# A decoder layer's attention loop with one PSUM bank for both heads' turned probabilities and two for the projections

## The reference

```
x = x + attn(layernorm(x))        # rmsnorm inside, 16 heads of 64, softmax in fp32, output projection + bias
x = x + xattn(ctx, ctx, layernorm(x))   # one head of 128: q from x, k and v from the context, softmax, Wo + bo
x = x + ffn(layernorm(x))         # 128 -> 512 -> 128, relu; uint8 activations, int8 weights per channel

quant_act_uint8(x):    s = max(max(x), 1e-8) / 255;  round(x / s) clipped to 0..255, times s
quant_weight_int8(w):  s per row = max(|w|) / 127;   bias rounded to multiples of s_in * s_w
```

## Time and profile before

| | |
|---|---|
| runs | 414.09, 414.68, 415.33 us; median 414.68 |
| profiled execution | 414.31 us, its span 412.1 us |
| busy | PE 376.0 (91%), DVE 320.0 (78%), ACT 260.4 (63%), POOL 161.0 (39%) |
| one middle batch | 44.5 us, from like rows of neighbouring batches |
| first scores of the batches' loop, last output projection | 14.4 us, 366 us |
| TensorE's granted clock | 1.00 in all middle batches; half for some 3 us in the first batch and for stretches after 382 us |

### The profile page before, as it was taken

One profiled execution on the slowest core, in us unless ns is written; L12 is line 12 of the kernel. 1 busy time (PEld: TensorE's weight loads), 2 busy tenths in 40 slices (PEclk: granted clock), 3 DMA queues, 4 the chain that ended last, 5 costly groups with the idle time before them and its releaser, 6 DMA issues.

```text
span 412.1 us, 9065 instructions
## 1 busy us (share of the span) xinstructions
PE 376.0 (91%) x2989; PEld 289.1 (70%) x2989; DVE 320.0 (78%) x779; ACT 260.4 (63%) x814; POOL 161.0 (39%) x177
## 2 busy tenths in 40 slices
PE   1799999999999999999999999999999989987746
PEld 1677877687767876887768777787678767765115
DVE  3587778877987798859887798779885979847883
ACT  3676567675657665766767665766576656825762
POOL 1255534453454353534445345435353443401000
PEclk9989999999999999999999999999999999999659
DMA  7400000001000010001000100001000000000003
GB/s 241 128 15 2 0 2 2 1 3 40 2 0 3 0 40 0 0 0 38 0 0 0 38 0 0 0 0 38 0 0 0 25 2 2 2 2 0 0 0 103
DMA packets 12310, 7.50 MB, mean 18 GB/s; under 512 B 1280, under 2 KB 11264, under 8 KB 12288
## 3 DMA queue, kind: packets, MB, share of 16 engines
q1 hardware_dynamic: 11856, 6.69, 5.5%
q10 hardware_dynamic: 432, 0.52, 0.4%
HBM read 6.16 MB, written 1.05 MB: 18 GB/s over the span
## 4 chain that ended last, share of the span: by engine, by line
PE 75%; DVE 10%; issue 8%; POOL 3%; ACT 2%; DMA 1%; DVEq 0%; POOLq 0%; ACTq 0%
PE o_bank L467 14%; PE pT L458 12%; PE score L448 12%; PE acc_bank L474 6%; PE q_bank L431 6%; PE q_bank L433 3%; PE q_bank L432 3%; PE side_bank L431 3%; PE side_bank L525 3%; PE side_bank L432 2%; PE side_bank L433 2%; DVE h_max L1211 2%; DVE negmax L889 2%; POOL rstd L1245 2%; PE side_bank L521 2%
## 5 line engine op out<-in xcount | busy, mean ns | idle before, releaser
L1254 POOL TENSOR_TENSOR prob<-prob,rinv 128x512 f32<-128x512 f32 x128 | 132.5, 1044 | 178.6 <-DVE rinv L893 178.6
L707 ACT ACTIVATE prob<-score,negmax 128x256 f32<-128x256 f32 x252 | 117.1, 475 | 79.1 <-DVE negmax L889 78.3
L889 DVE TENSOR_REDUCE negmax<-score 128x2 f32<-128x512 f32 x126 | 80.9, 683 | 43.7 <-PE score L448 43.6
L896 DVE COPY pT<-pT 128x512 f32<-128x512 f32 x128 | 86.3, 677 | 1.6
L458 PE MATMUL pT<-ident,prob 128*128 128x128 f32 x512 | 71.2, 282 | 0.1
L467 PE MATMUL o_bank<-pT,v_sb 128*64 128x256 f32 x512 | 69.4, 392 | 0.6 <-ACT oT L698 0.6
L458 PEld LDWEIGHTS pT<-ident,prob 128*128 128x128 f32 x512 | 55.6, 142 | 9.7 <-issue 0.9
L707 ACT ACTIVATION_READ_ACCUMULATOR prob<-score,negmax 128x1 f32 x252 | 51.8, 206 | 0.0
L698 ACT ACTIVATE q_hi<-q_bank 128x512 fp32r<-128x512 f32 x62 | 37.4, 604 | 18.4 <-PE q_bank L433 17.9
L448 PE MATMUL score<-q_hi 64*128 64x256 f32 x252 | 42.2, 330 | 2.1 <-ACT prob L707 2.1
L431 PE MATMUL q_bank<-ht_hi,wqk_hi 128*128 128x256 f32 x124 | 41.6, 335 | 2.3 <-DVE q_lo L881 1.2
(11 more groups left out here) (216 smaller groups left out, 599.9 us busy)
## 6 DMA issues: line engine op xcount, KB each, us to landing
c_sb<-in_ctx_dram SPq DMA_DIRECT2D x8, 256.0 KB, 2.8
x_sb<-in_x_dram SPq DMA_DIRECT2D x8, 128.0 KB, 2.6
out_dram<-xn_all SPq DMA_DIRECT2D x4, 256.0 KB, 2.5
big<-in_L_attn_wk_dram ACTq DMA_DIRECT2D x2, 256.0 KB, 4.4
big<-in_L_attn_wq_dram SPq DMA_DIRECT2D x2, 256.0 KB, 5.6
big<-in_L_attn_wv_dram SPq DMA_DIRECT2D x2, 256.0 KB, 6.1
wo_sb<-in_L_attn_w_out_dram SPq DMA_DIRECT2D x1, 512.0 KB, 7.6
w_sb<-in_L_ffn_w_dram SPq DMA_DIRECT2D x2, 256.0 KB, 4.6
```

Of the source, the lines that this page charges most:

```text
L707: last = nc.scalar.activation(prob[:, slot, t, :], banks[r][:, t * S:(t + 1) * S], ACT.Exp, bias=negmax[:, slot, t:t + 1], scale=1.0, accu ...
L889: nc.vector.tensor_reduce(negmax[:, slot], banks[r][:].rearrange("p (t k) -> p t k", k=S), X_AXIS, ALU.max, negate=True).then_inc(max_done, 1)
L896: nc.vector.tensor_copy(pT[:, slot].rearrange("p k q -> p (k q)"), pT_bank[r][:]).then_inc(pT_done, 1)
L1254: nc.gpsimd.tensor_tensor(prob[:, slot], prob[:, slot], rinv[:, slot].unsqueeze(2).to_broadcast([P, QT, S]), ALU.mult).then_inc(prob_done, 1)
```

## The change

- One bank, `turned_bank`, takes head 0's turned probabilities, is copied out, and takes head 1's. Head 1's turning stands behind the values. The bank that this frees is a second projection bank; q's low part is waited for ahead of the scores and not ahead of the projection.
- Order inside a step on TensorE: `project_out` comes ahead of the side task of place 1; pair 7's `project_out` stands ahead of pair 1's scores.
- Side tasks: V2 is gone, W2 does its work in its own batch at pair 0; UX0 and UX1 are one task of four matmuls over 256 columns; UX and OX of batch 6 are done in the last batch's steps and not behind them.
- VectorE: `residual` ahead of the maxima and `aggregate(1)` behind them at pair 1; norm 1's `normalise` at pair 3 and no longer at pair 0; the copy of head 0's turned probabilities ahead of `split_lo`; norm 3 of batch 6 inside the last batch; the feed-forward weights' scaling at pairs 0 and 3 of the last batch where it was at 2, 3 and 5. GpSimd: `inverse_root(1)` ahead of the scaling.
- Tail: the scale of the second matmul is applied by ScalarE with the bias, so that turning back is a plain transpose (`turn_back`); each second feed-forward matmul waits for its own tile.

```diff
@@ -49,17 +49,15 @@
-PLACE = {(0, 0): "TC", (0, 1): "W1", (1, 0): "W3", (1, 1): "TH", (2, 0): "V0", (2, 1): "TX", (3, 0): "QX",
-         (3, 1): "SX0", (4, 0): "SX1", (4, 1): "PX0", (5, 0): "PX1", (5, 1): "UX0", (6, 0): "UX1", (6, 1): "OX",
-         (7, 0): "V2"}
+PLACE = {(0, 0): "W2", (0, 1): "TC", (1, 0): "W1", (2, 0): "W3", (2, 1): "TX", (3, 0): "QX", (3, 1): "TH",
+         (4, 0): "SX0", (4, 1): "PX0", (5, 0): "SX1", (5, 1): "PX1", (6, 0): "UX", (6, 1): "OX", (7, 0): "V0"}
 PAIRS_PER_BATCH = 8
-PREPARE = ["TH", "V0", "V2"]
-OWN = ["W1", "W3"]
-AFTER_LAST = ["UX0", "UX1", "OX"]
-LAST_PLACE = {k: t for k, t in PLACE.items() if t not in [*PREPARE, *AFTER_LAST]}
-LAST_PLACE[6, 1] = "TL"
-LAST_PLACE |= {(PAIRS_PER_BATCH, n): t for n, t in enumerate(AFTER_LAST)}
+PREPARE = ["TH", "V0"]
+OWN = ["W1", "W2", "W3"]
+LAST_PLACE = {k: t for k, t in PLACE.items() if t not in PREPARE}
+LAST_PLACE[7, 0] = "TL"
 PLACES = {"first": {k: t for k, t in PLACE.items() if t in [*PREPARE, *OWN]}, "mid": PLACE, "last": LAST_PLACE}
 PLACES["first"] |= {(3, 0): "XW", (5, 0): "XE"}
...
@@ -234,15 +232,16 @@
         score_bank = [bank("score0"), bank("score1")]
-        pT_bank = [bank("pT0"), bank("pT1")]
-        q_bank = bank("q_bank")
+        turned_bank = bank("turned_bank")
+        q_banks = [bank("q_bank0"), bank("q_bank1")]
+        pT_bank = [turned_bank, q_banks[1]]
...
@@ -522,7 +521,8 @@
                                                    x_prob[:, int(task[2]), kt * P:(kt + 1) * P], ident[:])
                 elif task[:2] == "UX":
                     for kt in range(CT):
-                        last = nc.tensor.matmul(side_bank[:, 0:P], c_sb[:, p, kt, :], x_pT[:, kt, int(task[2]), :],
+                        last = nc.tensor.matmul(side_bank[:, 0:S], c_sb[:, p, kt, :],
+                                                x_pT[:, kt].rearrange("p t q -> p (t q)"),
                                                 start=(kt == 0), stop=(kt == CT - 1))
                 else:
                     for t in range(QT):
...
@@ -532,40 +532,43 @@
             def step(kind, b, parity, i, j):
                 g = b * PAIRS + j
-                more_q, more_scores = ahead(kind, j, 3), ahead(kind, j, 2)
-                if more_scores:
-                    pe.wait_ge(q_lo_done, g + 3)
+                more_q, more_scores, cross = ahead(kind, j, 3), ahead(kind, j, 2), kind != "first"
                 if kind == "first" and j == 1:
                     pe.wait_ge(wqk_lo_done, 4)
                 if more_q:
-                    project_qk((j + 3) % PAIRS, parity if j < PAIRS - 3 else 1 - parity)
+                    project_qk((j + 3) % PAIRS, parity if j < PAIRS - 3 else 1 - parity, q_banks[(j + 3) % 2])
                 if task := side_at(kind, j, 0):
                     side(kind, b, 1 - parity, i, task)
+                if cross and j == 1:
+                    pe.wait_ge(o_done, g - 1)
+                    project_out(PAIRS - 1)
                 if more_scores:
+                    pe.wait_ge(q_lo_done, g + 3)
                     pe.wait_ge(exp_done, 2 * g + 4)
                     scores(j % 2)
                 pe.wait_ge(prob_done, 2 * g + 1)
-                wait(pe, pT_done, 2 * g - 1)
-                turn_probs(0, 2 * j % 8)
-                pe.wait_ge(prob_done, 2 * g + 2)
                 wait(pe, pT_done, 2 * g)
-                turn_probs(1, 2 * j % 8 + 1)
-                if task := side_at(kind, j, 1):
-                    side(kind, b, 1 - parity, i, task)
+                turn_probs(2 * j % 8)
                 if not (kind == "first" and j < 1):
                     wait(pe, o_done, g - 1)
-                if not (kind == "first" and j < 2):
+                if j != 1 and not (kind == "first" and j < 2):
                     if j == 2:
                         wait(pe, x1_done, b)
                     if kind == "first" and j == 2:
                         pe.wait_ge(load_wo, 16)
                     project_out((j - 2) % PAIRS)
+                if task := side_at(kind, j, 1):
+                    side(kind, b, 1 - parity, i, task)
                 if not (kind == "first" and j < 1):
                     if j == 1:
-                        pe.wait_ge(side_free, side_before(kind, b))
+                        pe.wait_ge(side_free, side_index(kind, b, "W2") + 1)
                     slot = 2 * (j - 1) % 4
                     values((j - 1) % PAIRS, (slot, slot + 1), 1 - parity if j == 0 else parity)
+                pe.wait_ge(prob_done, 2 * g + 2)
+                pe.wait_ge(pT_done, 2 * g + 1)
+                turn_probs(2 * j % 8 + 1)
             pe.wait_ge(consts, 1)
...
@@ -593,9 +595,6 @@
             pe.wait_ge(o_done, B * PAIRS)
             project_out(PAIRS - 1)
-            for task in AFTER_LAST:
-                side("last", LAST, 1 - LAST % 2, LAST // 2, task)
             def turn_rows(dst, first, count):
                 for t in range(count):
...
@@ -669,27 +668,26 @@
             pe.wait_ge(h_done, CHUNKS * FT)
-            def scale_back(n):
+            def turn_back(n):
                 pe.wait_ge(yT_done, n + 1)
                 wait(pe, y_done, n - 1)
                 for k in range(4):
-                    last = nc.tensor.matmul(y_banks[n % 2][:, k * P:(k + 1) * P],
-                                            xrT[:, (4 * n + k) * P:(4 * n + k + 1) * P], s2_diag[:], start=True, stop=True)
+                    last = nc.tensor.transpose(y_banks[n % 2][:, k * P:(k + 1) * P],
+                                               xrT[:, (4 * n + k) * P:(4 * n + k + 1) * P], ident[:])
                 last.then_inc(y_raw, 1)
+            tiles_of = {True: 0, False: 0}
             for n in range(CHUNKS):
-                pe.wait_ge(hq_act, (3 * n + 1) // 2 + 1)
-                pe.wait_ge(hq_dve, 4 * (n + 1) - (3 * n + 1) // 2 - 1)
                 wait(pe, yT_done, n - 1)
                 for c in range(FT):
+                    tiles_of[by_act(n, c)] += 1
+                    pe.wait_ge(hq_act if by_act(n, c) else hq_dve, tiles_of[by_act(n, c)])
                     last = nc.tensor.matmul(yT_banks[n % 2][:], w2_qT[:, c, :], h_q[:, c, n * 512:(n + 1) * 512],
                                             start=(c == 0), stop=(c == FT - 1))
                 last.then_inc(yT_raw, 1)
-                if n == 1:
-                    pe.wait_ge(diag_done, 1)
                 if n >= 1:
-                    scale_back(n - 1)
-            scale_back(CHUNKS - 1)
+                    turn_back(n - 1)
+            turn_back(CHUNKS - 1)
         @block.scalar
...
@@ -759,8 +756,7 @@
-                if kind == "last" and j == 4:
+                if kind == "last" and j == 1:
                     act.wait_ge(w_inv_done, 1)
                     for c in range(FT):
                         copy(w_t[:, c * D:(c + 1) * D], w1_sb[:, c, :], bias=ROUND, scale=w_inv[:, c:c + 1])
...
@@ -871,7 +863,7 @@
             for n in range(CHUNKS):
                 act.wait_ge(yT_raw, n + 1)
                 nc.scalar.activation(xrT[:, n * 512:(n + 1) * 512], yT_banks[n % 2][:], ACT.Identity,
-                                     bias=b_col[:, FT:FT + 1], scale=1.0).then_inc(yT_done, 1)
+                                     bias=b2_scaled[:], scale=s2_col[:]).then_inc(yT_done, 1)
         @block.vector
...
@@ -1022,48 +1013,45 @@
                 if ahead(kind, j, 1):
                     dve.wait_ge(exp_done, 2 * g + 4)
                     invert_sums((2 * j + 3) % 8)
-                if kind == "mid" and j == PAIRS - 1:
+                if cross and j == PAIRS - 1:
                     aggregate(2, b, *PLAIN_NORM)
                 if prepare and j == 0:
                     dve.wait_ge(load_x[1 - parity], (i + 2) * 16)
                     statistics(0, tiles(x_sb[:, 1 - parity]), b + 2)
                 if cross and j == 2:
                     normalise(1, tiles(xn2), tiles(x1_sb), b, xn2_done)
+                if prepare and j == 3:
+                    normalise(0, tiles(xn1), tiles(x_sb[:, 1 - parity]), b + 2, xn1_done)
                 if task := side_at(kind, j, 0):
                     side(kind, b, 1 - parity, task)
+                if cross and j == 1:
+                    residual(b, 1 - parity)
                 if more_scores:
                     for r in range(2):
                         dve.wait_ge(score_raw, 2 * g + 5 + r)
                         maxima(r, (2 * j + 4 + r) % 8)
-                early = side_at(kind, j, 1) == "SX0"
-                if early:
-                    side(kind, b, 1 - parity, "SX0")
                 if prepare and j == 0:
                     aggregate(0, b + 2, *FIRST_NORM)
+                if cross and j == 1:
+                    aggregate(1, b, *PLAIN_NORM)
+                dve.wait_ge(pT_raw, 2 * g + 1)
+                keep_turned(2 * j % 4)
                 if ahead(kind, j, 3):
                     dve.wait_ge(q_hi_done, g + 4)
-                    split_lo((j + 3) % 2)
```

(36 more changed lines are left out.)

64 lines of the change are left out of this document (26 added, 38 removed).

## The result

The changed kernel takes **418.48 us** (median of 5 runs, 417.4 to 419.43) against 414.68 (5 runs, 413.84 to 415.33): ratio 1.0088, 95% interval 1.006 to 1.0115, so slower by 0.9%. The profiled execution has a span of 416.6 us instead of 412.1.

A forecast was written before the change was run, and what follows sets the result against it. TensorE was taken to bound the batches, latency the chain behind them. Terms: middle 2.0, first batch 0.9, its clock 0.6, last batch 3.3, cross tail 0, end -1.9, sum +4.9 on 414.31; forecast 419.4 us, range 414.0 to 423.5.

The forecast's parts named there:

- no wait at TX: Middle batches, pair 2: TensorE's 1.18 us wait for VectorE's normalisation, ahead of transposing the normalised rows, goes.
- a cheap u: Sign of being wrong: the joined u matmul takes about 1.0 us, against 1.9 assumed; it would give 0.9 a batch.
- The stall at pair 1: Middle batches: the second turning waits 1.21 us for VectorE's copy out of the shared bank.
- The small stalls: Middle batches, other pairs: shared-bank waits, 0.14 us in a step with no task behind the output projection; 0.3 per batch together.
- The turning cut in two could cost or save some 0.05 a step; I take 0: Middle batches, TensorE: splitting the two heads' turning was given no cost or saving.
- if the clock stays low until 3.8 us of work have been done again: First batch: turning, projection and W1 would run at half clock, 1.9 us; +0.6 taken between 0 and 1.9.
- the short holes of pairs 6 and 7: Last batch: TensorE's short holes, set against scaling of the last weights at 0.1 to 0.5 us, so neither was counted.
- -1.2 if the clock rises late: End of the kernel: smaller bound of the forecast gain of 1.9 us; the other bound was -2.4.
- First (no new wait): Rival: VectorE's copy at pair 1 is out in time, so no wait replaces pair 2's; 410.9 us, chance 0.15.
- Second (holes): Rival: 3.15 us of work moved into the last batch falls into holes, first-batch clock recovers in time; 415.5, chance 0.16.
- Third: Rival: VectorE falls behind in every step, a copy 0.1 us later in all 64; some +4, 423.5 us, chance 0.09.
- Fourth: Rival: TensorE's clock falls once in each middle batch, losing 1.65 us each, six times; 429 us, chance 0.03.

The follow-up runs named there:

- a2: Changed kernel with the variance of norm 2 behind the first copy at pair 1 instead of ahead of it; 415.21 us, ratio 1.0011.
- c4: c1 with the second turning behind the values and the output projection ahead of the second side task, plus a later copy wait; 407.86 us, ratio 0.9838.
- c1: Kernel before, two turned banks kept, with early output projection and norm, variance behind the copy, joined u and new end; 406.96 us, ratio 0.9805.
- c2: c1 with the second head's turning behind the values, in its own bank, plus a later copy wait; 414.21 us, ratio 0.9997.
- c3: c1 with the output projection ahead of the second side task instead of behind it; 409.29 us, ratio 0.9887.
- a3: Changed kernel with TensorE's two gaps in the first batch filled by repeated W2 matmuls and transposes; 416.67 us, ratio 1.0049.
- b2: Kernel before with only the new end: wait per tile, scale in ScalarE's copy, plain transposes back; 411.90 us, ratio 0.9933.
- a4: Changed kernel with u and OX of batch 6 behind the last batch's eighth pair again; 415.26 us, ratio 1.001.
- b1: Kernel before with only pair 7's output projection ahead of pair 1's scores and the early residual, variance and inverse root; 410.13 us, ratio 0.9891.
- a1: Changed kernel with a turned bank for each head and one projection bank again, q's low part split ahead of the first copy; 411.84 us, ratio 0.9936.

## Why the prediction came out right

The direction was right, and so was the mechanism of the main stall. The sum was right partly by luck, because its errors cancel: the middle batches came out 4.0 under the forecast, the four other terms together 3.6 over it.

| term | forecast | measured |
|---|---|---|
| six middle batches | +2.0 | -1.98 |
| first batch, with clock | +1.5 | +2.84 |
| last batch | +3.3 | +3.81 |
| cross tail | 0 | +0.83 |
| end | -1.9 | -1.00 |
| sum | +4.9 | +4.5 |

Of the prediction's own signs of being right two came: no wait at TX, and 1.14 ahead of the second turning of pair 1, with VectorE's copy as releaser. Three did not: the batch period is 0.33 shorter and not 0.3 longer, the last output projection is 4.65 later (364.75 and 369.40) and not 5 or more, and the last add is 0.2 nearer to it and not 1.9. One of its signs of being wrong came, the shorter batch period; a cheap u did not (1.81, forecast 1.9). Its last step also has a slip: 419.2 and 0.4 are 419.6, not 419.4, which changes nothing here.

**Middle batches.** The stall at pair 1 was forecast at 1.21 and is 1.14; a2 took exactly the variance's part out of it. The wait for the norm went, as said. The small stalls are larger than forecast: in the table of pieces TensorE's idle time is 1.39 a batch, and 0.39 more than before stands inside the values' column, in waits too short for a bracket, so 1.78 a batch against the forecast's 1.51. In before the idle time is 1.02, where the forecast took 1.18 away. So the waits alone cost +0.76 a batch, not +0.33. The step that failed is "The turning cut in two could cost or save some 0.05 a step; I take 0", together with taking the output projection at its old 0.54 in a new place. The turnings are 0.39 a batch cheaper, the output projections 0.56, the projections 0.20, the side tasks 0.12 dearer: -1.03 a batch. The two together give -0.27 in this stretch; -0.33 was measured over all six. c4 against c1 confirms the sign on another base, at a smaller size (-0.18 a batch). c2 and c3 add that no piece has a saving of its own: it depends on what stands behind it. What inside TensorE makes a group cheaper ahead of one neighbour than ahead of another stays open.

**First batch.** The forecast took 0.6 for the clock, on "if the clock stays low until 3.8 us of work have been done again". That failed: it stood at half for 7.81 us of work, with an idle stretch of 2.39 in their midst. a3 prices it at 1.60, within the bound of 1.9, on single executions, of which b2 shows how much they vary. Less that and the start's 0.19, 1.05 remain for the idle time, forecast at 0.9.

**Last batch.** The size holds, not its parts. u and OX cost 1.19 there (a4), not 2.36, since part of them lies in waits. In their place stands what the prediction let cancel as "the short holes of pairs 6 and 7": the new order with its late second turning, 1.98 on c1's base (the later wait of c4 included). The scaling of the last weights, priced at 0.1 to 0.5 with no row, fits: the stall at pair 1 is 1.26 in the last batch and 1.06 in the others by the brackets. That these parts add up to 3.81 is not shown; they were measured on two bases.

**Cross tail and end.** The prediction saw that TensorE would idle 3 us there and set +0.9 of clock against -0.9 of an earlier transpose. Only the clock came (+0.83; a4, which filled the gap, takes 0.89 back). The end's -1.9 is what b2 measured (-1.94); in the changed kernel 0.9 of it is lost to a clock that rose late, which the prediction had as the bound "-1.2 if the clock rises late". Since kernels with the same end differ by up to 0.9 there, the close agreement of b2 is partly luck too.

**The rivals.** First (no new wait): refuted at its own point, a stall of 1.14 against 0.35. But b1 and a1, kernels without the shared bank, came out near its 410.9 (410.1 and 411.8). Second (holes): half right, for u. Third: no; the small stalls are some 0.3 a batch over the forecast, which is 2 us in all, and the cheaper pieces outweigh them. Fourth: the clock did not fall in the middle.

## What to carry to other kernels

When one bank serves two uses in turn, count both sides from one event: when the writer comes back, and how long the reader's whole queue takes up to the copy. A wait that goes in one place and comes back as a wait for a bank is no gain; the early norm with a bank for each use kept most of it (b1: 410.1 from 414.7).

Price a moved piece by its start to the next start in its new neighbourhood, not by its old one: 0.05 us at 8 places in 8 batches are 3 us. But c2 to c4 show that such terms do not add up by themselves. Check a new order by the piece that it brings forward: what it reads, and who has its bank. And when an order is tried on its own, let each wait ask for no more than its own bank needs.

An idle stretch of TensorE can have two prices, its length and a stretch at half clock behind it. Work that is off the chain can still be worth its place, if it fills such a gap.

## What the runs showed of the hardware

- After an idle stretch of 2.87 us TensorE's granted clock fell to half and, with one more gap of 2.39 us in it, stayed there from 20.5 to 30.7. After 2.13 idle in before it stood at half for some 3.4 us; in b2, after the same 2.13 and with the same code there, for 6.9. In a3, with the first gap filled, an idle stretch of 2.57 us left it at 1.00. So the length of one gap alone did not decide.
- The clock at the end of the program differed between kernels with the same end: from the start of the last quantisation it stood at half for 3.6 to 6.3 us, and the stage took 12.34 to 13.28.
- Some 1.4 us of idle time in each middle batch, with PSUM banks used in turn, left the clock at 1.00 (after).
- Four fp32 transposes take 0.49 of the stream ahead of an output projection and 0.38 to 0.42 ahead of a projection; four fp32 matmuls of the output projection 0.44 ahead of a side task of transposes and 0.54 ahead of 64-column values.
- Eight fp32 instructions of 256 columns take 1.01 for the values, whose weights have 64 columns, and 1.81 for the joined u, whose weights have 128.
- ScalarE's copy of 128x512 with a scale per partition took 0.77, without one 0.67.
